# Two more semaphore waits ahead of the GpSimd scatters in the expert block loop

## What is computed

```
scores = sigmoid(xt @ gate_w.T)
_, idx = top_k(scores + gate_b, 4)
w = take(scores, idx); w = w / sum(w) * 2.5
comb = zeros((T, 16)).at[arange(T)[:, None], idx].add(w)
for e in range(16):
    h = silu_and_mul(xt @ w13[e].T)
    y = y + comb[:, e, None] * (h @ w2[e].T)
y = y + silu_and_mul(xt @ w13_s.T) @ w2_s.T
```

## Time and profile before

| | us |
|---|---|
| runs | 1906.38, 1903.9, 1902.3 |
| median | 1903.9 |
| profiled execution, its own time | 1903.56 |
| its span, first to last instruction | 1901.8 |
| PE busy of the span | 1550.4 (82%) |
| DVE busy | 1423.9 (75%) |
| ACT busy | 1092.2 (57%) |
| POOL busy | 1042.6 (55%) |

### The profile page before, as it was taken

How to read it: one execution, slowest core, us unless ns; L and a number is a source line. 1 busy time by engine, 2 the same in 40 slices (tenths; PEclk the granted TensorE clock), 3 DMA queues, 4 the chain that set the end, 5 groups by cost and what they waited for, 6 DMA issues and landing times. The chain is left out here.

```text
span 1901.8 us, 35726 instructions
## 1 busy us (share of the span) xinstructions
PE 1550.4 (82%) x10562; PEld 1321.7 (69%) x10562; DVE 1423.9 (75%) x3336; ACT 1092.2 (57%) x2311; POOL 1042.6 (55%) x940
## 2 busy tenths in 40 slices
PE   6749999988888988989898894178888887875798
PEld 4337788777777777777777774067777777775565
DVE  6747899999999999999999995434444444442688
ACT  4635766767767676767676764245555545453222
POOL 2113446566666666666666666725555555554553
PEclk9879999999999999999999996589999999997899
DMA  8620011212121212122121215555555555552998
GB/s 283 211 80 32 25 49 43 79 60 79 62 80 61 80 59 72 64 71 71 61 77 62 75 56 171 187 168 157 168 155 159 154 171 149 162 152 75 373 400 322
DMA packets 149368, 238.24 MB, mean 125 GB/s; under 512 B 27792, under 2 KB 96144, under 8 KB 149008
## 3 DMA queue, kind: packets, MB, share of 16 engines
q1 hardware_dynamic: 123296, 166.20, 27.7%
q0 software_dynamic: 25344, 69.50, 9.9%
q10 hardware_dynamic: 544, 0.26, 0.0%
HBM read 128.66 MB, written 109.35 MB: 125 GB/s over the span
## 5 line engine op out<-in xcount | busy, mean ns | idle before, releaser
L2270 POOL DMA_INDIRECT ys_dram<-byo,bids x272 | 261.7, 962 | 256.3 <-DVE bids L2250 155.1
L1625 DVE SCALAR_TENSOR_TENSOR cv<-xc,convw,cv 128x256 f32<-128x256 f32 x576 | 331.0, 629 | 14.1 <-ACT xc L1476 14.1
L1105 POOL DMA_INDIRECT xs_dram<-rows,dest x256 | 264.5, 1033 | 61.5 <-issue 59.2
L2223 DVE TENSOR_TENSOR bhl<-bank,bhh 128x512 fp32r<-128x512 f32 x136 | 94.1, 692 | 195.9 <-ACT bhh L2175 185.0
L116 PE MATMUL bank<-wh,bhh 128*128 x544 | 161.0, 296 | 77.3 <-ACT bhh L2175 63.6
L2175 ACT ACTIVATE bhh<-bank 128x512 fp32r<-128x512 f32 x136 | 83.5, 614 | 185.2 <-PE bank L2108 177.3
L116 PEld LDWEIGHTS bank<-wh,bhh 128*128 128x128 f32 x544 | 103.0, 189 | 90.7 <-issue 90.7
L117 PE MATMUL bank<-wl,bhh 128*128 x544 | 154.9, 285 | 1.5 <-issue 1.5
L118 PE MATMUL bank<-wh,bhl 128*128 x544 | 154.0, 283 | 0.9 <-issue 0.9
L1945 POOL TENSOR_TENSOR state<-state,par 128x512 f32<-128x512 f32 x64 | 94.7, 1479 | 104.5 <-PE bank L1326 104.4
L116 PE MATMUL bank<-hTh,win_hi 128*128 128x256 f32 x384 | 114.5, 298 | 32.1 <-DVE xr L1745 21.4
(11 more groups left out here) (269 smaller groups left out, 5400.0 us busy)
## 6 DMA issues: line engine op xcount, KB each, us to landing
bx<-xs_dram SPq DMA_DIRECT2D x272, 129.0 KB
cy<-ys_dram SPq DMA_DIRECT2D x32, 1024.0 KB, 13.1
px<-in_x SPq DMA_DIRECT2D x16, 512.0 KB, 6.0
h_t<-phT SPq DMA_DIRECT2D x16, 512.0 KB, 3.7
hT<-h_t SPq DMA_DIRECT2D x32, 256.0 KB
xr<-in_x SPq DMA_DIRECT2D x32, 256.0 KB
x_dram<-xr SPq DMA_DIRECT2D x32, 256.0 KB
h_dram<-h SPq DMA_DIRECT2D x32, 256.0 KB
```

The costliest lines, as they stand in the source:

```text
L1105: pool.indirect_dma_start(out=xs_dram[:, :], out_offset=bass.IndirectOffsetOnAxis(ap=dest[p][:, CH * b + c, k:k + 1], axis=0), in_=rows[b] ...
L1625: dve.scalar_tensor_tensor(cv[b][:, m, :], xc[b][:, m, tap:tap + GROUP], convw[:, m, tap:tap + 1], cv[b][:, m, :], ALU.mult, ALU.add).then ...
L2223: dve.tensor_tensor(hl[u % 2][:, :, :, :].rearrange("p k n t -> p (k n t)"), XT[u % 2][:, :], hh[u % 2][:, :, :, :].rearrange("p k n t -> ...
L2270: pool.indirect_dma_start(out=ys_dram[:, :], out_offset=bass.IndirectOffsetOnAxis(ap=ids[u % XBUF][:, n:n + 1], axis=0), in_=yo[u % YBUF][ ...
```

## The change

Ahead of each of the two scatters of a pair, POOL waits for one more count. The first scatter of pair u waits until the down product of pair u + 1 has ended; the second waits until the up product of pair u + 4 has. Near the end of the loop both are capped at the last count. No instruction that computes or moves data is added, removed or put in another place.

```diff
                     pool.wait_ge(yo_done, u + 1)
                     pool.wait_ge(ids_done, u + 1)
                     for n in range(2):
+                        if n == 0:
+                            pool.wait_ge(down_ps, min(u + 2, PAIRS))
+                        else:
+                            pool.wait_ge(up_ps, min(u + 5, PAIRS))
                         pool.indirect_dma_start(
                             out=ys_dram[:, :],
                             out_offset=bass.IndirectOffsetOnAxis(ap=ids[u % XBUF][:, n:n + 1], axis=0),
```

## The result

| | us |
|---|---|
| before | 1903.1 (4 runs, 1898.96 to 1906.38) |
| with the two waits | 1846.64 (4 runs, 1844.03 to 1851.08) |
| ratio | 0.9707, 95% interval 0.968 to 0.9734 |
| profiled execution, time and span | 1844.03, 1841.9 |

Forecast was 1826 with a range of 1785 to 1878. The change is faster by 2.9%, 56 us; the forecast was 77 us faster.

The account below looks back on a forecast made before the run. PE bounds the steady loop but loses a fifth of its time to late signals. From 1903.56 us, 130 pairs x (3.65 - 3.05) = 78 us less, landing and tail costed at nothing, gives 1826; range 1785 to 1878.

Parts of the forecast that it names:

- The cause: Steady loop: while one scatter follows another, PE's completion signals are held until some 1.6 to 2.0 us after the last started.
- rival C: Nothing changes: holding has another cause, say the loads of `bx`, or POOL's waits are met anyway; 1904 us, chance 0.07.
- a rule against this: PE's signals: the skill's semaphore-tail model gives some 56 ns a signal, so nothing to win and 1904 us.
- A hold of up to about 2 us costs PE nothing.: PE's loop: turn runs two pairs ahead, leaving 2.2 us of cover, which the present 3.47 us exceed.
- The run is cut.: POOL's scatters: one whose signal is held cannot start, so runs of four at 1.27 us end; holding need not vanish.
- the two waits being met in turn: POOL's waits: one scatter after a down, one after an up, never two upon one signal; 1.37 or 1.42 us apart.
- three scatters in 1.27 + 1.27 + 2.07 = 4.61 us are 3.07 a pair. I take 3.05: Steady loop's pace: one scatter in three meets a held signal; 3.65 falls to 3.05 us a pair, 78 us less.
- rival B: Signals held in every pair, every second scatter late: 3.34 us a pair, 40 us less, 1863; chance 0.14.
- The tail: Loop's end: POOL, 12.7 us behind the last up product, would be 10 to 12 behind, eight scatters left; costed at 0.
- The landing: take_y's wait for both scatters of a pair to land: now once, 0.3 us; costed at nothing.
- Rival A: Holding goes altogether, if neighbours need 1.27 and not 1.37 us: 2.79 us a pair, 112 us less, 1792; chance 0.25.
- Rival D: Slower: a lone scatter holds signals too, POOL and PE wait in turn; 4.14 us a pair, 64 us more, 1967; chance 0.12.

Follow-up runs that it names:

- direct_pool: Kernel before the change, with the two scatters of each pair replaced by plain stores of the same bytes on POOL's queue; 1785.91 us, ratio 0.9376.
- no_scatter: All scatters of the loop and the waits for their landing left out, combine reading as many bytes from input x; 1772.49 us, one run.
- lone: Second scatter of every pair left out, without the added waits, combine reading from input x; 1786.89 us, one run.

## Why the prediction was right, and where its size was off

**The cause.** Right, and now shown: scatters in a row hold PE's signals. Without scatters no signal is late and PE is never idle, and the same bytes as plain stores hold nothing. "The loads of `bx`" and "nothing", rival C, are out. The prediction set a rule against this. It stands in the Trainium skill, "TensorE: Matmul & The Clock Gate", section "The cost: per-tile semaphore tail" (the prediction names another page for it), and models the tail of a signal as 25 ns, 4.7 for each tile and 26.3 for each increment. Without scatters signals come 0.01 us behind the modelled end, and the trace is within the rule. With scatters in a row one was answered 3.47 us behind it in the earlier trace rows, and there the rule, by which there was nothing to win, isn't borne out. The Trainium skill, "SBUF — State Buffer", section "SBUF: two separate sides", which says that DMA and compute do not slow each other, was put beside rival C. The trace agrees with it in `direct_pool` and with lone scatters, where PE is busy all 300 us; scatters in a row did slow PE, though its matmuls themselves ran on and only their signals came late.

**"A hold of up to about 2 us costs PE nothing."** It held for the transposes: in the changed kernel L2175 never waits for them. The gain isn't fewer held signals (0.99 of them are held, more than before) but shorter holding. It did not hold for the whole. The up product's signal is about 2.0 us late in nearly every pair, and a pair takes 3.21 us against the 2.80 of `no_scatter`. How the late signal reaches PE can be read from the trace, though no run tests it. Ahead of the up product the weight loads stand idle 101 times in the 109 pairs, 0.33 us a pair:

```profile
PEld bank L116 <- issue: 35.9, 101, 0.7
```

Before that, PE's sequencer stands at the waits of `down` (L2138) for 314 ns in the median, where it passes in 51 ns without scatters. It is let go 0.04 us behind the end of DVE's `bfl`, which comes late because `bgs` waited for the up product's signal (L2182 at 1503.81, `bfl` until 1504.98, the wait until 1505.02). Next the sequencer loads the next pair's weight offsets (L2146), 657 ns here and 537 without scatters. Without scatters it is early enough for that load to pass while matmuls run; here PE runs dry behind it. The same lines, changed kernel and then `no_scatter`, 1300 to 1600 us (ns min/median/max):

```profile
L2138 PEldq EVENT_SEMAPHORE  x93: 51/314/413, 1301.8 to 1597.6; - x93
L2146 PEldq TENSOR_LOAD <-weights_at x94: 537/657/934, 1299.4 to 1598.5; - x94
```

```profile
L2138 PEldq EVENT_SEMAPHORE  x108: 51/51/120, 1300.2 to 1599.8; - x108
L2146 PEldq TENSOR_LOAD <-weights_at x107: 532/537/551, 1300.9 to 1597.7; - x107
```

**"The run is cut."** Right in the effect: runs of two, not four. The description of the two waits being met in turn was wrong. In the steady part one burst meets both, the second wait first; the second wait alone gives the whole gain (`second_only`), the first alone under half of it (`first_only`, 0.9866).

**The term that was mis-sized** is the pace, "three scatters in 1.27 + 1.27 + 2.07 = 4.61 us are 3.07 a pair. I take 3.05". The step that failed is "a scatter that starts 2.07 behind the last has no neighbour, so that signals behind it are prompt, and PE's lead lets the next two follow". It has a neighbour, the one that starts 1.26 us after it, and the signals between were held already: the up product that ended 0.94 us behind the scatter at 1504.05 came out with the rest. So each burst frees two scatters and no third one. That is the pattern of rival B, 1.27 + 2.07 = 3.34 us, where the long spacing measured some 1.94, so 3.21: signals come out 1.70 us behind the last scatter and not 1.94 (again 0.03 off ACT's start), and POOL starts 0.27 behind that and not 0.13. The 0.13 does not follow from the last `byo`, as the prediction has it: that ended at 1503.82, 0.28 before the scatter at 1504.10. With 130 x (3.65 - 3.21) = 57 us the sum would have given 1846 or 1847. The chance stood at the wrong place: 0.42 for the forecast's band of 2.9 to 3.2 us a pair, 1806 to 1845, which the result missed by a little, and 0.14 for two in every cycle. The forecast's sign and cause were reasoned and came true; that the range held the result owes something to rival B having been taken into it.

**The tail** was costed at 0, between 10 and 12 us behind the last up product; it is 14.0, and cost 1.3 us. Ten scatters were left behind the last up product and not eight, and one of them stood 2.05 us for a down product (1685.97). **The landing** of scatters was costed at nothing, and the changed kernel's byo rows have it once, 0.3 us, as before. **Rival A** would have needed spacings over 1.57 us, which 2.8 us a pair cannot give. **Rival D** is refuted by `lone`. Of the signs that were named, the wait of L2175, PE's share (0.95, over 0.93) and the end of the runs of four came as stated; "spacings between 1.3 and 2.1" came as 1.26, which is under it, and 1.94.

## What to carry to other kernels

Where an engine waits long for a matmul that the timeline shows as ended, look at what else runs in that time: the signal may be late, not the work. Then ask how much lead the waiting work has: here 2.2 us of cover hid a hold of 1.9 us and not one of 3.47. Queue order alone can cost: a wait added to an engine with time to spare cut bursts of scatters and made the whole 2.9% faster, although it added nothing but waiting. Where results could be stored in order and gathered later, a plain store in the scatter's place is worth more (2.80 us a pair against 3.21), and should be weighed against what the gather costs, which no run here measured.

## What the runs showed of the hardware

Indirect DMAs issued by GpSimd within 1.27 to 1.57 us of each other delayed the semaphore signals of PE's completions. The signals came out some 1.6 to 2.0 us after the start of the last scatter where the spacing was 1.27, and 1.35 to 1.5 us after the start of one where it was 1.49 or 1.57. Signals of ACT and DVE in the same stretch were prompt: in the kernel before, from 1300 to 1600 us, none of the 496 that have a record came more than 0.012 us behind its instruction's end (`bgs` ended at 1506.16 and DVE started its product at 1506.20). At 1.68 us, or with one every 2.8 us, or with plain stores, no signal or next to none was delayed. PE itself went on with its matmuls during the delay. What path the signals share with the scatters, why the edge lies between 1.57 and 1.68 us, and what sets the moment at which they come out, stays open: the runs show when it happens and not by what. The cycle of 1.26 + 1.94 us between POOL and the held signals accounts for the changed kernel's pace on POOL's side; on PE's side it is the late `bfl` and the load of offsets behind it, as read above from one trace and not tested by a run.
